# First mixer of a two-layer graph transformer: two heads' features by 64-row matmuls in turn, values with both halves as the stationary operand, and the next pair's key projection inside a pair

## The chip, the cores and the metric

The kernel runs on one core of one Trainium2 chip. The metric is the device time of one execution, in microseconds (us). Five engines work beside each other, each through its own list of instructions: PE (TensorE: matmuls; PEld is its weight load), DVE (VectorE), ACT (ScalarE), POOL (GpSimd) and SP (SyncE, which here only issues DMAs). They meet at semaphores. PSUM, into which PE writes, has eight banks.

## The reference, cut to what matters

625 nodes of 768 features pass through two layers, each of a graph network plus a mixer, and then a mixture of eight experts. The change touches only the first layer's mixer:

```python
xn = layernorm(x)                                    # 625 x 768
qkv = (xn @ W_qkv + b_qkv).reshape(b, n, 3, 12, 64)  # q, k, v: 12 heads of 64
q, k = q / 8, k / 8
phi_q = relu(einsum('bhnd,md->bhnm', q, random_features))   # 256 features
phi_k = relu(einsum('bhnd,md->bhnm', k, random_features))
kv   = einsum('bhnm,bhnd->bhmd', phi_k, v)
attn = einsum('bhnm,bhmd->bhnd', phi_q, kv) / 256
out  = attn.reshape(b, n, 768) @ W_proj + b_proj
```

## The kernel before, in words

**Arithmetic.** Every float32 product is made of three matmuls on two-part operands: a value is split in a high part (rounded by the write to the fp32r type) and a low part (the rest), and `mm3` (L582 to L588) adds high×high (L584), high×low (L587) and low×high (L588). So each operand is made by two engines in turn: ACT writes the high part out of PSUM, DVE subtracts it for the low part. Weights are split in a like way by POOL in this stage: `split` (L756) waits for the raw weights' DMA and until PE has used the unit two before (semaphore `unit_used`), writes the high part (L764) and then the low part (L766), which raises `unit_ready`. There are two buffers for units.

**The stage.** Nodes are five tiles of 128 (the last has 113 rows). XT holds the normalised rows transposed. The values of all heads are made first, in ten products of 18 matmuls, and kept as node rows in `attnT` (L1397, L1403, L915). Then a loop runs over six pairs of heads; a pair is 128 columns of q and of k. For each pair PE does, in this order (L2143 on):
- the projections of keys and queries: 4 × 18 matmuls with 320 moving columns, out of two weight units of 128 columns (2j and 2j+1; it waits for both before it begins), into banks 0 to 3. Then it tells POOL with `used(2)` (L2053) that both are free;
- for head s = 0, 1: the features of the keys (5 tiles × 3 matmuls, 256 columns each, banks 4 and 5) and of the queries (4 × 3 matmuls, 320 columns, banks 0 to 3). The random features are stored per head with zeros in the other head's 64 rows (`rfT[:, s, :]`), so that every matmul is one of 128 rows;
- `key_values`: phi_k (stationary, 128 nodes × 128 features) times the values of both heads (128 moving columns), for 2 feature halves × 5 tiles × 3 matmuls; of the result only the head's own 64 columns are kept;
- `attention`: 2 × 2 × 3 matmuls of 320 columns per head into banks 6 and 7; head 0's stand among head 1's features, head 1's at the end of the pair.

ACT and DVE follow each with its high and low part. In the names of the trace, `xt<-` and `weight<-` are the operands of a projection, `rfT` and `kT` (or `qT`) of the features, `attnT` and `phi_k` of key_values, `phi_qT` and `kv` of attention.

**What POOL does meanwhile.** The edges of the graph are sorted in this stage. DVE computes each edge's place (`pos_i`, L1375); after it, POOL goes through L802 on: it splits one 128-column unit, then issues eight indirect DMAs (L806) that scatter 125 edges each, then the next unit, until 80 scatters are done (behind the tenth unit); units 10 and 11 follow. Then it splits the two units of the output projection (`U_PROJ`). The sorted edges are read back by SP after the last scatter (L674).

**After the loop** PE waits for the last pair's `attnT` low part (L1438), does the output projection (`products(PR_PROJ, ...)`, 10 tiles × 18 matmuls of 384 columns), then the graph network.

Of the kernel before, what the change touches and what calls it, by code (L numbers as in the profile page):

```python
# [121 lines left out]
def build(nc, a, out):  # L122
    with ExitStack() as ctx:
# [67 lines left out]
        XN = er("xn_rows", [P, TILES, DIM], F32)  # L191
        rf2 = er("rf2", [P, 2, P], F32)
        rfT = er2("rfT", [P, 2, FEATS])
# [7 lines left out]
        with ExitStack() as here:  # L201
            srt, _ = allocator(here)
            src_i = srt("src_i", [EDGE_ROWS, EDGE_COLS], I32)
# [27 lines left out]
        with ExitStack() as here:  # L231
            mx, mx2 = allocator(here)
            attnT = mx2("attnT", [P, KD, COLS])
            qT = mx2("qT", [P, COLS])
            kT = mx2("kT", [P, COLS])
            v_f = [mx(f"v_f{s}", [P, WCOL], F32) for s in range(2)]
# [328 lines left out]
        FREE_A, FREE_B, FREE_C = 4, 2, 2  # L565
# [24 lines left out]
        def at(pair, *idx):  # L590
            return pair[0][idx], pair[1][idx]

# [47 lines left out]
        def _(sp):  # L640
# [115 lines left out]
        def _(pool):  # L756
# [31 lines left out]
            for part in rfT:  # L788
                pool.memset(f32(part[:, :, :]), 0.0).then_inc(consts, 1)
            pool.wait_ge(consts, 16)  # L790
# [25 lines left out]
            def expert_rows(n):  # L816
# [11 lines left out]
                pool.wait_ge(consts, 16 + 9 * (n + 1))  # L828
# [46 lines left out]
        def _(act):  # L875
# [28 lines left out]
            for s in range(2):  # L904
                own = slice(s * HEAD0, (s + 1) * HEAD0)
                act.activation(rfT[0][own, s, :], ps[own, RF_BANK, 0:FEATS], ACT.Copy).then_inc(rf_hi, 1)
            end_phase(act, "act", 1)

            act.wait_ge(consts, 16)
            act.dma_start(slot_rows_dram.rearrange("(s p) d -> p s d", p=P), zero_row[:, :].unsqueeze(1).broadcast_to([P, XSLOTS, DIM])).then_inc(cleared, 16)  # L910

            for j in range(SET):
                col, t = j // TILES, j % TILES
                act.wait_ge(prod_used, PR_V0 + j + 1)
                act.activation(attnT[0][:, 3 * col:3 * col + 3, t * P:(t + 1) * P], v_f[j % 2][:, :].rearrange("p (k n) -> p k n", k=3), ACT.Copy).then_inc(v_hi, 1)  # L915
            def key_features(j, s, n):
                t = slice(2 * n, min(2 * n + 2, TILES))
                w = t.stop - t.start
                act.wait_ge(B_full, 8 * j + 4 * s + n + 1)
                act.activation(phi_k[0][:, t, :], ps[:, 4 + n % 2, 0:w * FEATS].rearrange("p (t m) -> p t m", t=w), ACT.Relu).then_inc(B_hi, 1)  # L920

            def query_features(j, s, n):
                act.wait_ge(A_full, 12 * j + 4 * s + 2 * n + 6)
                act.activation(halves(phi_qT[0][:, n, :]), ps[:, 2 * n:2 * n + 2, 0:HALF], ACT.Relu).then_inc(A_hi, 2)

            with act.Fori(0, PAIRS) as j:
                for n in range(2):

                    act.wait_ge(A_full, 12 * j + 2 * n + 2)
                    act.activation(halves((kT, qT)[n][0][:, :]), ps[:, 2 * n:2 * n + 2, 0:HALF], ACT.Identity,  # L930
                                   bias=qk_bias[:, ds((1 - n) * KD + j, 1)]).then_inc(A_hi, 2)
                for s in range(2):
                    key_features(j, s, 0)
                    key_features(j, s, 1)
                    query_features(j, s, 0)
                    key_features(j, s, 2)
                    query_features(j, s, 1)
                    act.wait_ge(B_full, 8 * j + 4 * s + 4)
# [1597 lines left out]
```

## Time and profile before

| | us |
|---|---|
| three runs | 2519.56, 2531.16, 2527.87 |
| their median | 2527.87 |
| the profiled execution: own time | 2522.39 |
| its span in the trace | 2520.7 |
| mean granted clock of TensorE over the span | 0.935 of full |

The profiled execution lies 5.5 us below the median. Times in the trace count from the start of its span. A row of a timeline has: start, duration, engine, line, operation, output<-inputs, shapes, and in brackets the engine's idle time just before it with what ended it.

### The profile page before, as it was taken

To read this page: it belongs to the slowest core of one execution; us is meant where nothing else is said; L and a number is where in the kernel's file an instruction comes from. 1 tells how busy PE (TensorE), PEld (TensorE's weight loads), DVE (VectorE), ACT (ScalarE), POOL (GpSimd) and SP (SyncE) were. 2 spreads that over 40 slices of the span, in tenths; PEclk is the share of its full clock that TensorE was granted. 3 is DMA by queue.
4 is the path that set the end of the run, shared out by engine and by line. 5 is a ranking of instruction groups with operands and counts; after the bars stand their busy time and mean duration, and the time that the engine had idled before them with its cause. 6 is when DMAs were issued, how large, how long until landed. Compare 5 with 4: busy or idle time off the path is not lost. (4 is left out here: it accounts for less than half of the span.)

```text
span 2520.7 us, 33797 instructions
## 1 busy us (share of the span) xinstructions
PE 2216.7 (88%) x13346; PEld 2117.9 (84%) x13346; DVE 1408.4 (56%) x2284; ACT 942.0 (37%) x1250; POOL 500.7 (20%) x256
## 2 busy tenths in 40 slices
PE   5899999999999999999869919868888868999995
PEld 4899999999999999999858819767778857999995
DVE  7533455554555133333458863257984576888885
ACT  1222246666333011112126612214512223776772
POOL 4885510000300443443010012201110001000001
PEclk9899999999899999999969969988889977999997
DMA  3411223332322111110159951100112027999995
GB/s 99 133 26 52 69 86 128 112 125 93 140 94 85 57 51 44 38 57 20 48 176 308 299 194 38 63 28 30 53 59 84 13 91 266 350 348 360 346 338 186
DMA packets 158185, 326.79 MB, mean 130 GB/s; under 512 B 14096, under 2 KB 99296, under 8 KB 158042
## 3 DMA queue, kind: packets, MB, share of 16 engines
q1 hardware_dynamic: 133354, 265.68, 30.8%
q10 hardware_dynamic: 18928, 43.27, 4.8%
q0 software_dynamic: 5760, 15.86, 2.0%
q8 instruction: 98, 1.61, 0.3%
q14 instruction: 45, 0.37, 0.0%
HBM read 278.19 MB, written 46.51 MB: 129 GB/s over the span
## 5 line engine op out<-in xcount | busy, mean ns | idle before, releaser
L584 PE MATMUL banks<-weight_hi,xt_hi 128*128 128x384 f32 (+2 forms) x2208 | 740.9, 336 | 56.7 <-DVE xt_lo L1299 11.8
L587 PE MATMUL banks<-weight_lo,xt_hi 128*128 128x384 f32 (+2 forms) x2208 | 723.4, 328 | 0.0
L588 PE MATMUL banks<-weight_hi,xt_lo 128*128 128x384 f32 (+2 forms) x2208 | 723.0, 327 | 0.0
L584 PEld LDWEIGHTS banks<-weight_hi,xt_hi 128*128 128x128 f32 x2208 | 427.7, 194 | 72.9 <-issue 19.6
L587 PEld LDWEIGHTS banks<-weight_lo,xt_hi 128*128 128x128 f32 x2208 | 427.7, 194 | 0.4 <-issue 0.2
L588 PEld LDWEIGHTS banks<-weight_hi,xt_lo 128*128 128x128 f32 x2208 | 427.2, 193 | 0.0
L1704 DVE TENSOR_TENSOR weight_lo<-weight_raw,weight_hi 128x2304 fp32r<-128x2304 f32 (+2 forms) x153 | 342.5, 2243 | 89.3 <-ACT weight_hi L1039 89.3
L1039 ACT ACTIVATE weight_hi<-weight_raw 128x2304 fp32r<-128x2304 f32 (+2 forms) x153 | 287.0, 1879 | 71.4 <-PE banks L584 46.1
L764 POOL TENSOR_TENSOR weight_hi<-weight_raw,zero_col 128x2304 fp32r<-128x2304 f32 (+1 forms) x36 | 120.0, 3333 | 771.0 <-PE banks L584 334.3
L2220 PE MATMUL banks<-held_hi,a_rel 128*128 128x384 f32 x550 | 189.3, 344 | 0.6 <-DVE held_lo L1485 0.6
L2220 PE MATMUL banks<-held_lo,a_rel 128*128 128x384 f32 x550 | 187.6, 341 | 0.0
L584 PE MATMUL banks<-weight_hi,hT_hi 128*128 128x384 f32 (+1 forms) x442 | 151.2, 342 | 12.1 <-DVE hT_lo L1714 12.1
L1479 DVE TENSOR_TENSOR held_lo<-banks,held_hi 128x384 fp32r<-128x384 f32 x80 | 44.6, 557 | 209.5 <-ACT held_hi L977 209.5
L766 POOL TENSOR_TENSOR weight_lo<-weight_raw,weight_hi 128x2304 fp32r<-128x2304 f32 (+1 forms) x36 | 154.8, 4300 | 2.8
L588 PE MATMUL banks<-weight_hi,hT_lo 128*128 128x384 f32 (+1 forms) x442 | 149.7, 339 | 0.0
L587 PE MATMUL banks<-weight_lo,hT_hi 128*128 128x384 f32 (+1 forms) x442 | 149.7, 339 | 0.0
L866 POOL TENSOR_TENSOR weight_lo<-weight_raw,weight_hi 128x1536 fp32r<-128x1536 f32 (+2 forms) x16 | 70.3, 4393 | 350.6 <-ACT weight_hi L1100 350.6
L1467 DVE TENSOR_TENSOR adj<-adj,banks 128x640 f32 x80 | 65.4, 818 | 116.2 <-PE banks L2192 116.2
L977 ACT ACTIVATE held_hi<-banks 128x384 fp32r<-128x384 f32 x80 | 39.3, 491 | 242.2 <-PE banks L588 242.2
L853 POOL DMA_INDIRECT xt_hi<-slot_out,place x10 | 10.8, 1081 | 591.2 <-DMA slot_out<-bias_rows 588.8
L989 ACT ACTIVATE a_rel<-adj 128x640 fp32r<-128x640 uint16 x80 | 58.4, 744 | 173.1 <-PE banks L2220 173.1
L2220 PEld LDWEIGHTS banks<-held_hi,a_rel 128*128 128x128 f32 x550 | 105.3, 191 | 0.7 <-DVE held_lo L1485 0.7
(378 smaller groups left out, 4006.0 us busy)
## 6 DMA issues: line engine op xcount, KB each, us to landing
weight_raw<-L_ffn_w_in SPq DMA_DIRECT2D x102, 1152.0 KB, 6.4
weight_raw<-L_gnn_W_in SPq DMA_DIRECT2D x32, 1152.0 KB, 5.7
weight_raw<-L_ffn_W_in SPq DMA_DIRECT2D x17, 1152.0 KB, 7.3
products<-bias_rows SPq DMA_DIRECT2D x80, 192.0 KB, 1.9
slot_in<-slot_rows ACTq DMA_DIRECT2D x34, 384.0 KB, 6.2
slot_out<-bias_rows ACTq DMA_DIRECT2D x34, 384.0 KB, 5.8
weight_raw<-L_ffn_W_in SPq DMA_DIRECT2D x17, 576.0 KB, 6.2
product_back<-products SPq DMA_DIRECT2D x10, 960.0 KB, 4.7
```

The source lines that it names most:

```text
L584: ins = pe.matmul(dst, s[0], m[0], start=start, stop=False)
L587: pe.matmul(dst, s[0], m[1], start=False, stop=False)
L588: return pe.matmul(dst, s[1], m[0], start=False, stop=stop)
L764: pool.tensor_tensor(hi, raw[s][0:rows, 0:n], zero_col[0:rows, :].broadcast_to([rows, n]), ALU.add).then_inc(hi_ready, 1)
L766: pool.tensor_tensor(lo, raw[s][0:rows, 0:n], f32(hi), ALU.subtract).then_inc(unit_ready, 1)
L866: pool.tensor_tensor(lo, raw[u.slot][:, 0:n], f32(hi), ALU.subtract).then_inc(unit_ready, 1)
L989: act.activation(A_r[:, t, :, :], adj[:, r * TILES:(r + 1) * TILES, t * P:(t + 1) * P], ACT.Copy).then_inc(a_ready, 1)
L1039: act.activation(W4[u % RING][0][0:rows, 0:k * cols], RAW4[u % RAWS][0:rows, 0:k * cols], ACT.Copy).then_inc(e_hi[n], 1)
L1467: vec.tensor_tensor(block_of, block_of, ps[:, 2 * (s % 2):2 * (s % 2) + 2, 0:HALF], ALU.add).then_inc(slot_done, 1)
L1479: vec.tensor_tensor(lo[:, t, :], ps[:, part_bank(1, n), 0:WCOL], f32(hi[:, t, :]), ALU.subtract).then_inc(part_lo, 1)
L1704: vec.tensor_tensor(lo, RAW4[u % RAWS][0:rows, 0:k * cols], f32(hi), ALU.subtract).then_inc(e_lo[n], 1)
L2220: ins = pe.matmul(ps[:, agg_bank(m), 0:WCOL], A_r[:, t, src, :], part[:, src, :], start=(src == 0 and i == 0), stop=(src == FULL and i == 1))
```

## The change

1. `rfT` loses its zero halves (`[P, 2, FEATS]` becomes `[P, FEATS]`): the head s = 0 uses partitions 0 to 63, s = 1 uses 64 to 127, in matmuls of 64 rows. `heads3` issues them in turn: head 0, head 1, head 0, ... , each head into a bank of its own. Keys' and queries' features of both heads are read out together, by fewer and larger ACT and DVE instructions. Two memsets of POOL, one ACT and one DVE instruction go before the loop.
2. The values are stored so that one stationary operand of 128 columns holds head s's high half and low half side by side (`value_cols`). `keys_values` makes kv transposed, with phi_k as the moving operand: 2 heads × 5 tiles × 2 (phi_k high, phi_k low) matmuls of 256 columns. ACT copies the result out (512 columns), PE transposes it back by four 128×128 transposes, and DVE adds the parts and splits them (four instructions of 256 columns that wait for each other).
3. The order inside a pair is new, and written out instead of looped: the keys' projection of pair j+1 stands inside pair j, before the last two query features; the projection of the queries stands among the keys' features. Unit 2j is now the keys', 2j+1 the queries', each waited for by itself and freed by itself. POOL's list is as before.
4. XN moves to the part of SBUF that the sort uses; the wait counts on `consts` fall from 16 to 14.

```diff
-        rfT = er2("rfT", [P, 2, FEATS])
+        rfT = er2("rfT", [P, FEATS])
...
-            phi_k = mx2("phi_k", [P, TILES, FEATS])
-            phi_qT = mx2("phi_qT", [P, 2, COLS])
-            kv = mx2("kv", [P, 2, 2, P])
+            phi_k = mx2("phi_k", [P, 2, TILES, FEATS])
+            phi_qT = mx2("phi_qT", [P, 2, 2, COLS])
+            kv = mx2("kv", [P, 4 * P + 2 * HEAD0])
...
+        K_BANKS, Q_BANKS, F_BANKS, O_BANKS = slice(0, 2), slice(2, 4), slice(4, 6), slice(6, 8)
+        KEY_TILES = [slice(0, 2), slice(2, 4), slice(4, TILES)]
+        KEY_BANKS = [F_BANKS, K_BANKS, F_BANKS]
+        QUERY_BANKS = [F_BANKS, Q_BANKS]
...
-            with sp.Fori(0, PAIRS) as j:
+            for j in range(PAIRS):
                 for c in range(2):
-                    load(Unit(U_MIX + c, j, 2), qkv[:, :, c, ds(j * P, P)])
+                    load(Unit(U_MIX + 2 * j + c), qkv[:, :, 1 - c, j * P:(j + 1) * P])
... (ACT)
+            projection(0, 0)
+            for j in range(PAIRS):
+                for n in range(3):
+                    key_features(j, n)
+                projection(1, j)
+                act.wait_ge(B_full, 5 * j + 4)
+                act.activation(kvT_f, ps[:, O_BANKS.start, 0:2 * FEATS], ACT.Copy).then_inc(B_hi, 1)
+                for g in range(3):
+                    query_features(j, g)
+                if j + 1 < PAIRS:
+                    projection(0, j + 1)
+                query_features(j, 3)
... (DVE)
+            def keys_values(j):
+                of_hi, of_lo = kv_parts(O_BANKS.start + 1)
+                part = kv_part.rearrange("p (s m d) -> p s m d", s=2, m=2)
+                vec.wait_ge(B_full, 5 * j + 5)
+                order.step(vec.tensor_copy(part, of_lo))
+                order.wait()
+                order.step(vec.tensor_tensor(part, of_hi, part, ALU.add))
+                order.wait()
+                order.step(vec.tensor_copy(kv_own(kv[0]), part))
+                order.wait()
+                vec.tensor_tensor(kv_own(kv[1]), part, kv_own(f32(kv[0][:, :])), ALU.subtract).then_inc(B_done, 1)
... (DVE order: 3 key_features, projection(1, j), 2 query_features, keys_values, query_features, projection(0, j + 1), query_features, attention)
... (PE)
+            def heads3(bank, cols, of, by, unit_done):
+                for i, (a_of, a_by) in enumerate(((0, 0), (0, 1), (1, 0))):
+                    for s in range(2):
+                        own = slice(s * HEAD0, (s + 1) * HEAD0)
+                        ins = pe.matmul(ps[:, bank.start + s, cols], of[a_of][own], by[a_by][own], start=(i == 0), stop=(i == 2))
+                        if unit_done and i == 0 and s == 0:
+                            ins.then_inc(unit_used, 1)
+                return ins
...
+            def keys_values(j):
+                for s in range(2):
+                    for t in range(TILES):
+                        rows_of = slice(0, LAST if t == FULL else P)
+                        for h in range(2):
+                            ins = pe.matmul(ps[:, O_BANKS.start, s * FEATS:(s + 1) * FEATS], attnT[s][rows_of, j, t * P:(t + 1) * P],
+                                            phi_k[h][rows_of, s, t, :], start=(t == 0 and h == 0), stop=(t == FULL and h == 1))
+                            if s == 0 and t == 0 and h == 0:
+                                ins.then_inc(unit_used, 1)
+                ins.then_inc(B_full, 1)
...
+            for half in range(2):
+                projection(0, 0, half)
+            for j in range(PAIRS):
+                pe.wait_ge(A_done, 2 * j + 1)
+                if j > 0:
+                    pe.wait_ge(C_done, 5 * (j - 1) + 3)
+                key_features(j, 0, j == 0)
+                key_features(j, 1)
+                if j > 0:
+                    pe.wait_ge(C_done, 5 * (j - 1) + 4)
+                projection(1, j, 0)
+                pe.wait_ge(B_done, 4 * j + 1)
+                key_features(j, 2)
+                projection(1, j, 1)
+                if j == 0:
+                    pe.wait_ge(v_lo, SET)
+                else:
+                    pe.wait_ge(C_done, 5 * j)
+                pe.wait_ge(B_done, 4 * j + 3)
+                keys_values(j)
+                pe.wait_ge(A_done, 2 * j + 2)
+                query_features(j, 0)
+                query_features(j, 1)
+                pe.wait_ge(B_hi, 4 * j + 4)
+                for g in range(4):
+                    ins = pe.transpose(ps[:, O_BANKS.start + 1, g * P:(g + 1) * P], kvT_f[:, g * P:(g + 1) * P], ident[:, :])
+                ins.then_inc(B_full, 1)
+                if j + 1 < PAIRS:
+                    projection(0, j + 1, 0)
+                pe.wait_ge(C_done, 5 * j + 1)
+                query_features(j, 2)
+                if j + 1 < PAIRS:
+                    projection(0, j + 1, 1)
+                pe.wait_ge(C_done, 5 * j + 2)
+                query_features(j, 3, j + 1 < PAIRS)
+                pe.wait_ge(B_done, 4 * j + 4)
+                attention(j, 0)
+                pe.wait_ge(C_done, 5 * j + 4)
+                attention(j, 1).then_inc(C_full, 1)
+            pe.wait_ge(C_done, 5 * PAIRS)
             products(PR_PROJ, U_PROJ, lambda k: (attnT, k))
```

## Rows read from the trace of the kernel before

**Rows 1.** Busy time by stretch: us, then PE, PEld, DVE, ACT, POOL, granted clock, DMA
```profile
86.00:275.40 189.40, 177.46 (x1261) 172.19 (x1261) 59.43 (x92) 51.58 (x90) 135.70 (x96) 0.97 0.21 54
275.40:320.00 44.60, 43.85 (x251) 43.56 (x252) 21.61 (x25) 6.32 (x8) 22.09 (x5) 1.00 0.22 68
```

**Rows 2.** Timeline of ACT and DVE: keys of pairs 0, 4, 5; last result
```profile
93.69 0.80 ACT L930 ACTIVATE kT_hi<-banks,qk_bias 128x640 fp32r<-128x640 f32 x1 [8.89 <-PE banks L588]
217.60 0.80 ACT L930 ACTIVATE kT_hi<-banks,qk_bias 128x640 fp32r<-128x640 f32 x1 [4.58 <-PE banks L588]
247.65 0.80 ACT L930 ACTIVATE kT_hi<-banks,qk_bias 128x640 fp32r<-128x640 f32 x1 [4.58 <-PE banks L588]
274.50 0.82 DVE L1438 SCALAR_TENSOR_TENSOR attnT_lo<-banks,attnT_hi 128x640 f32 x1 [4.36 <-ACT attnT_hi L942]
```

**Rows 3.** Timeline of PE: first and last of four runs of one kind
```profile
99.83 0.28 PE L587 MATMUL banks<-rfT_lo,kT_hi 128*128 128x256 f32 x1
100.66 0.28 PE L588 MATMUL banks<-rfT_hi,kT_lo 128*128 128x256 f32 x1
103.14 0.22 PE L584 MATMUL banks<-attnT_hi,phi_k_hi 128*128 x1
106.33 0.27 PE L588 MATMUL banks<-attnT_hi,phi_k_lo 113*128 x1
146.59 0.41 PE L584 MATMUL banks<-phi_qT_hi,kv_hi 128*128 128x320 f32 x1 [0.77 <-DVE kv_lo L1434]
146.84 0.31 PE L587 MATMUL banks<-phi_qT_lo,kv_hi 128*128 128x320 f32 x1
150.29 0.31 PE L584 MATMUL banks<-xt_hi,weight_hi 128*128 128x320 f32 x1 [1.68 <-POOL weight_lo L766]
155.86 0.31 PE L588 MATMUL banks<-xt_hi,weight_lo 128*128 128x320 f32 x1
```

**Rows 4.** Timeline of POOL: splits and scatters of the loop
```profile
62.74 4.59 POOL L764 TENSOR_TENSOR weight_hi<-weight_raw,zero_col 128x768 fp32r<-128x768 f32 x1 [27.44 <-DVE pos_i L1375]
99.03 1.46 POOL L764 TENSOR_TENSOR weight_hi<-weight_raw,zero_col 128x768 fp32r<-128x768 f32 x1 [1.91 <-PEq L2053]
129.35 1.47 POOL L764 TENSOR_TENSOR weight_hi<-weight_raw,zero_col 128x768 fp32r<-128x768 f32 x1
192.81 1.46 POOL L764 TENSOR_TENSOR weight_hi<-weight_raw,zero_col 128x768 fp32r<-128x768 f32 x1 [0.75 <-PEq L2053]
222.50 1.19 POOL L806 DMA_INDIRECT edges_sorted<-code_i,pos_i  x1 [2.36 <-issue]
226.75 1.84 POOL L766 TENSOR_TENSOR weight_lo<-weight_raw,weight_hi 128x768 fp32r<-128x768 f32 x1
230.09 1.84 POOL L766 TENSOR_TENSOR weight_lo<-weight_raw,weight_hi 128x768 fp32r<-128x768 f32 x1
```

**Rows 5.** Granted clock in short stretches (columns as in rows 1)
```profile
86.00:88.00 2.00, 1.42 (x5) 1.42 (x6) 0.14 (x1) 0.00 (x0) 1.70 (x2) 0.50 0.99 334
178.00:182.00 4.00, 3.50 (x13) 3.51 (x14) 0.29 (x1) 0.04 (x1) 3.44 (x3) 0.57 0.05 13
```

**Rows 6.** Groups by line and form, 60 to 330 us: busy us, mean ns | idle
```profile
L1412 DVE SCALAR_TENSOR_TENSOR phi_k_lo<-banks,phi_k_hi 128x512 fp32r<-128x512 f32 x24 | 16.6, 691 | 17.8 <-ACT phi_k_hi L920 17.4
L924 ACT ACTIVATE phi_qT_hi<-banks 128x640 fp32r<-128x640 f32 x24 | 16.9, 705 | 9.1 <-PE banks L588 9.1
L1417 DVE SCALAR_TENSOR_TENSOR phi_qT_lo<-banks,phi_qT_hi 128x640 fp32r<-128x640 f32 x24 | 19.8, 824 | 8.2 <-ACT phi_qT_hi L924 7.8
L1412 DVE SCALAR_TENSOR_TENSOR phi_k_lo<-banks,phi_k_hi 128x256 fp32r<-128x256 f32 x12 | 5.0, 413 | 0.0
L584 PEld LDWEIGHTS banks<-attnT_hi,phi_k_hi 113*128 113x128 f32 x24 | 4.6, 192 | 0.1
```

**Rows 7.** Timeline before the loop (DVE) and at its start (PE)
```profile
32.54 0.88 DVE L1330 TENSOR_TENSOR rfT_lo<-banks,rfT_hi 64x256 fp32r<-64x256 f32 x2 [1.66 <-ACT rfT_hi L906]
...
86.58 0.63 PE L584 MATMUL banks<-xt_hi,weight_hi 128*128 128x320 f32 x1 [6.09 <-DVE attnT_lo L1403]
```

More of the change, by code:

```diff
@@ L922, in query_features @@
[L922 to L938, printed above, removed]
-                    act.activation(kv[0][:, :, s, s * HEAD0:(s + 1) * HEAD0], ps[:, 5, 0:2 * P].rearrange("p (m d) -> p m d", m=2)[:, :, s * HEAD0:(s + 1) * HEAD0],
-                                   ACT.Copy).then_inc(B_hi, 1)
-                act.wait_ge(C_full, 2 * j + 2)
-                act.activation(attnT[0][:, ds(j, 1), :].rearrange("p k (h n) -> p (k h) n", h=2), ps[:, 6:8, 0:HALF], ACT.Copy,
-                               scale=MIX0_SCALE).then_inc(C_hi, 1)
@@ L1326, in _ @@
             transposes_lo(TR_0)
[L1327 to L1330 removed]
+            vec.wait_ge(rf_hi, 1)
+            order.step(vec.tensor_tensor(rfT[1][:, :], ps[:, RF_BANK, 0:FEATS], f32(rfT[0][:, :]), ALU.subtract))
             vec.wait_ge(edges_in, 48)
@@ new lines, in _, with projection @@
+                    hi, lo = [value_cols(col, t, h) for h in range(2)]
+                    vec.tensor_tensor(lo, by_head(v_f[m % 2]), f32(hi), ALU.subtract).then_inc(v_lo, 1)
+            def projection(n, j):
+                t = (kT, qT)[n]
+                vec.wait_ge(A_hi, 2 * j + n + 1)
+                vec.scalar_tensor_tensor(halves(t[1][:, :]), ps[:, (K_BANKS, Q_BANKS)[n], 0:HALF], qk_bias[:, (1 - n) * KD + j:(1 - n) * KD + j + 1],
+                                         halves(f32(t[0][:, :])), ALU.add, ALU.subtract).then_inc(A_done, 1)
@@ new lines, in _ @@
+            projection(0, 0)
+            for j in range(PAIRS):
+                for n in range(3):
+                    key_features(j, n)
+                projection(1, j)
+                for g in range(2):
+                    query_features(j, g)
+                keys_values(j)
+                query_features(j, 2)
+                if j + 1 < PAIRS:
+                    projection(0, j + 1)
+                query_features(j, 3)
+                hi, lo = [halves(t[:, j, :]) for t in attnT]
+                vec.wait_ge(C_hi, 5 * j + 5)
+                vec.scalar_tensor_tensor(lo, ps[:, O_BANKS, 0:HALF], MIX0_SCALE, f32(hi), ALU.mult, ALU.subtract).then_inc(C_done, 1)
@@ L2163, in _, with projection @@
-            pe.wait_ge(C_done, FREE_C + 2 * PAIRS)
+            def projection(n, j, half):
+                u = U_MIX + 2 * j + n
+                pe.wait_ge(unit_ready, u + 1)
+                w = unit_view(u % 2, KD, P)
+                for k in range(KD):
+                    ins = mm3(pe, ps[:, (K_BANKS, Q_BANKS)[n].start + half, 0:HALF], at(w, slice(None), k), at(XT, slice(None), k, cols_half(half)),
+                              k == 0, k == KD - 1)
+                ins.then_inc(A_full, 1)
@@ new lines, in key_features, with query_features @@
+            def key_features(j, n, unit_done=False):
+                tiles = KEY_TILES[n]
+                for t in range(tiles.start, tiles.stop):
+                    i = t - tiles.start
+                    ins = heads3(KEY_BANKS[n], slice(i * FEATS, (i + 1) * FEATS), at(kT, slice(None), slice(t * P, (t + 1) * P)), rfT,
+                                 unit_done and i == 0)
+                ins.then_inc(B_full, 1)
+            def query_features(j, g, unit_done=False):
+                half, m = g // 2, g % 2
+                heads3(QUERY_BANKS[m], slice(0, HALF), at(rfT, slice(None), slice(m * P, (m + 1) * P)), at(qT, slice(None), cols_half(half)),
+                       unit_done).then_inc(C_full, 1)
```

172 lines of the change are left out of this document (58 added, 114 removed).

## The prediction

> **What bounds the kernel now.** I read the busy time by stretch first. The loop over the pairs of heads runs from about 86 to 275.4 us; PE is busy 177.5 of 189.4 us there, but POOL is busy too, 135.7 us, while DVE and ACT have less than a third [rows 1]. So there are two candidates, and the timelines have to tell which of them holds the end. After the loop PE is busy 43.9 of 44.6 us [rows 1]: what the loop gains is kept by what follows, since the weight splits there are released by PE's own progress.
>
> PE's pace: from pair 4's to pair 5's keys on ACT it is 247.65 − 217.60 = 30.05 us per pair [rows 2]. How that is made up comes from the starts of matmuls (their listed durations overlap). 39 rows of 320 columns in one run give 5.57 / 38 = 0.147 us from start to start; eight of 256 columns give 0.83 / 7 = 0.119; thirty of key_values, 128 columns, give 3.19 / 29 = 0.110 [rows 3]. From 320 to 256 columns 0.028 us go, so 128 columns would come to about 0.06; the 0.110 is a floor of another kind, which I read as the pace of the weight loads. A pair is then 72 × 0.147 = 10.6 (projections), 30 × 0.119 = 3.6 (key features), 24 × 0.147 = 3.5 (query features), 60 × 0.110 = 6.6 (key_values) and 24 × 0.147 = 3.5 (attention): 27.8, plus some 2.2 us of waits, such as the 0.77 for kv's low part [rows 3].
>
> POOL's pace: between the first splits of units 2 and 4 lie 129.35 − 99.03 = 30.3 us [rows 4], two splits and 16 scatters. It is nearly PE's pace. In the whole loop POOL waited for PE only 1.91 + 0.75 us; the other gaps, like the 2.36 at a scatter, have "issue" as their cause and are its own [rows 4]. In pair 2 PE waited 1.68 us for POOL [rows 3]. **So the two run neck and neck, and a faster PE meets POOL's list.** Unit 10 is ready at 226.75 + 1.84 = 228.6, unit 11 at 231.9 [rows 4].
>
> **The change part by part.**
> - *key_values.* 60 matmuls at 0.110 become 20 of 256 columns at 0.119: 6.6 − 2.4 = 4.2 us less per pair. Four transposes of 128 columns come: between the 0.110 of a 128-column matmul and the 0.25 of a restart; nearer the first, 0.15 each, 0.6 us [rows 3].
> - *64-row matmuls.* Their number (54 per pair) and columns stay. No row has one of 64 rows in turn with another. The nearest: the 113-row matmuls of key_values, mixed with 128-row ones, keep the 0.110 pace [rows 3], so fewer rows alone neither cost nor save. I take the old prices, 7.1 us per pair. Below: the 0.110 pace, 5.9. Further below: both heads at once, half of 7.1. Above: each changeover costs what a restart after a wait costs, 0.25 instead of 0.147 [rows 3]; with some ten changes between 64 and 128 rows per pair, 1.0 us, which I count.
> - *Order.* The waits at the start of a pair (keys' features for kT's low part, POOL's signal through a drain) are covered by the attention and the next projection. PE alone would need 10.6 + 7.1 + 2.4 + 0.6 + 3.5 + 1.0 = 25.2 us per pair, some 5 less than now.
> - *ACT and DVE.* Same elements in fewer instructions. DVE per pair: 1.8 (projections), key features of 1024, 1024 and 512 elements at 1.08 ns each from 0.691 and 0.413 [rows 6], 2.9, query features 4 × 0.82, kv four of about 0.4, attention 0.8: about 10.4 us, hidden under 25. It costs only where a chain is open, at the end.
> - *POOL.* Its list in the loop is unchanged. Its two waits for PE go, 2.7 us, because key units are freed by each pair's last query features and query units by keys_values, at least 10 us before POOL asks. The sort starts a bit sooner: rfT's two instructions of 0.44 each on DVE and as many on ACT become one each, 0.8 us [rows 7]. The two memsets lie beside an early wait for DMA: nothing. Later PE's first projection may begin when the values' products are read, not 6.09 us after [rows 7]; that too is nothing at the end, since the loop is paced by POOL.
> - *SP.* The loads keep place, size and number; keys' and queries' columns change turns. Written out loops cost code loading; PE's other stages are written out and are busy: nothing. After the loop U_PROJ's first unit is freed in pair 4, its second at pair 5's keys_values, about 247 plus 9.2 us of split: before it is needed, 16 us into the projection.
>
> **What the path is then.** POOL gives unit 10 (pair 5's keys) at 228.6 − 2.7 − 0.8 = 225.1 and unit 11 at 228.4. PE, with unit 9 at 207.8 (half of 30.3 and the 2.1 us that the pause at a scatter lasts over the usual 0.3, before unit 10), does pair 4's query projection, the last key features, keys_values, two query features and transposes in 5.3 + 0.7 + 2.4 + 1.8 + 0.6 = 10.8 us and stands at 219; it then **waits 6 us in front of pair 5's key projection**. This wait takes the place of the gain. From 225.2: key projection 7.1 (after an idle of 6.09 us the same 36 matmuls went from 86.58 to ACT's 93.69, partly at half clock, instead of 5.3) [rows 2, 5, 7]; two query features 1.8; attention 3.5 and 0.3 for its last query feature; key features 2.9; query projection 5.3; key features of the last tile 0.7; keys_values 2.4; query features 1.8: 251.0. Then the open chain of the last pair, no next projection to cover it: ACT and DVE on a query feature 0.7 + 0.8 [rows 6], DVE's four steps for kv 2.0, two more query features on DVE 1.6, attention's last half 0.4 + 1.8, ACT and DVE on the result 1.6: 8.9. Some 13 changeovers at 0.1: 1.3. The loop ends at 261.2, against 274.50 + 0.82 = 275.3 [rows 2]: **14.1 us less**. The profiled execution (2522.4) would go to 2508.3; it lies 5.5 us under the median, so against 2527.9 I forecast 2513.8.
>
> A measurement of this kernel can tell about 0.5%, 12.6 us, from no change; the forecast lies just past it.
>
> **Rivals.**
> 1. *The heads really run at once.* Then 24 key and 24 query-feature matmuls and the last tile's between 225 and the end (42 in all, 5.6 us) halve: 2.8 us more, a gain of 17, 2511. Nothing in the trace speaks for it, since no 64-row matmul is there; nor against. In pairs before the last it only makes the wait for POOL longer. The Trainium skill, "TensorE: Matmul & The Clock Gate", Part 3, The mechanism, states that matmuls in different row groups overlap, starting about 4 ns apart; by it this rival is the case. Chance 0.2.
> 2. *Nothing to tell.* PE's changeovers cost more, or its clock falls. In 178 to 182 us the granted clock was 0.57 though PE was 3.5 of 4 us busy, right after key_values [rows 5]: half of the time at 1.2 instead of 2.4 GHz, without a real pause. With half-filled matmuls and a wait in each pair this can come twice more on the way from 225 to the end: 2 × 1.8 = 3.6 us; and changeovers at 0.35 instead of 0.1 add 13 × 0.25 = 3.3. The gain is 7: 2521. The skill, "TensorEngine Tiling (Array Packing)", Key Properties, says that a change of tiling mode drains TensorE, without a price; no row here shows one. Chance 0.28.
> 3. *POOL does not hold PE.* If the scatters went faster than I read, the end would be PE's: a start at 84 (part of the 6.09 us wait before 86.58 goes [rows 7]) + 1.8 for the half clock + 6 × 25.2 + some 7 of the last pair's open chain = 244, a gain of 31, 2497. Against it is POOL's unchanged list with hardly a wait [rows 4]. Chance 0.04.
> 4. *Slower: the changing halves break the overlap of weight load and matmul in the features.* Its place is `heads3`. A 64-row load for one half might wait for the other half's matmul; each of 54 matmuls per pair would then cost load and matmul one after the other, 0.19 + 0.28 = 0.47 instead of 0.13, 18 us per pair [rows 3, 6]. PE would need 43 us per pair and the loop end near 350: 75 us slower, 2603. The point from which it decides: the end passes 275 when a pair takes over 30.5 us of PE, that is 0.1 us more for each of the 54. The unbroken 0.110 pace with 113-row loads speaks against it [rows 3]. Chance 0.06.
>
> That the change does not do what it says can only be rival 1's half of it: "in turn" need not be "at once".
>
> **How the numbers follow.** The forecast has 0.42; with rival 1 (0.20), 2 (0.28), 3 (0.04), 4 (0.06) that is all. Of the forecast's own 0.42, some 0.11 falls short of 12.6 us, because it lies 1.5 us past that bound. Faster by over 0.5%: 0.31 + 0.19 + 0.04 = 0.54; within: 0.11 + 0.28 + 0.01 = 0.40; slower: 0.06. The range goes from rival 1's gain with the runs' own spread below the median (8 us, 2519.56 against 2527.87) to rival 2's with the 3 us above: 2503 to 2524, widened at the top to 2526 for a gain of 5. Rivals 3 and 4 are left out.
>
> **What the profile would show.** POOL's scatters and splits without a wait for PE in the loop, unit 11 split by 228.5. PE waiting for POOL's low part before key projections, the last time about 6 us until 225, and clock 0.5 to 0.6 right after it. Matmul starts in the features 0.12 to 0.15 us apart (rival 1: in pairs with next to nothing between; rival 4: 0.4 and more). keys_values 2.4 us. The last attnT low part ending near 261. From there on every stage the same length as before. I am wrong if PE waits for nothing at the pairs' borders, or if the loop's gain is taken back later by a transfer or split that does not move with PE.

## Result, and the profile after the change

| | before | after |
|---|---|---|
| median of 5 runs each, us | 2523.71 (2519.56 to 2531.16) | 2506.35 (2503.13 to 2508.38) |
| ratio, 95% interval | | 0.9925 [0.9904, 0.9947] |
| profiled execution: own time, span, us | 2522.4, 2520.7 | 2508.38, 2506.6 |
| end of the last attention result, us | 275.32 | 265.57 |

The kernel is faster by 0.75%, 17.4 us; forecast were 14.1 us and a median of 2513.8. Between the two profiled executions lie 2520.7 − 2506.6 = 14.1 us of span. That equality with the forecast is luck: the loop gave only 275.32 − 265.57 = 9.75 us. The rest came in stages that the change does not touch. One line's instructions, in the expert stage, before and then after (first and last start):

```profile
L1722 DVE COPY bias_rows<-banks x68: 545/548/558, 1325.4 to 2493.5; 128x384 f32<-128x384 f32 x68
```

```profile
L1765 DVE COPY bias_rows<-banks x68: 546/549/558, 1321.1 to 2479.4; 128x384 f32<-128x384 f32 x68
```

At its first copy the changed kernel is 4.3 us ahead, at its last 14.1. So in this pair of executions the unchanged stages took away 5.4 us of the loop's gain and gave 9.8 us back later. With the repeats below, the change gave 0.75%, 0.35% and 0.54%, and the stretch behind the loop is no shorter with it; what a single profile shows there is scatter. I therefore go by the end of the loop from here on, and by the medians only for the whole.

Busy time by stretch, after (columns as in [rows 1]):

```profile
86.00:265.60 179.60, 147.65 (x1041) 134.19 (x1039) 69.60 (x87) 48.26 (x66) 136.38 (x96) 0.91 0.24 61
265.60:310.30 44.70, 43.92 (x248) 43.63 (x249) 21.13 (x24) 6.33 (x8) 21.53 (x5) 1.00 0.19 57
227.00:229.00 2.00, 2.00 (x8) 2.00 (x9) 0.00 (x0) 0.00 (x0) 1.92 (x2) 0.50 0.45 80
258.00:260.00 2.00, 1.98 (x7) 1.98 (x8) 1.43 (x2) 0.00 (x0) 0.00 (x0) 0.50 0.70 161
```

PE was busy in all but 12 us of the loop [rows 1]; now 32 us of it are idle. POOL's busy time is the same, 136.4 against 135.7 us, in a loop 9.8 us shorter. The granted clock fell from 0.97 to 0.91. The stretch behind the loop is as full as before. Who is waited for at the borders of pairs is shown by PE's timeline, and POOL's has the other side:

```profile
194.34 0.43 PE L592 MATMUL banks<-xt_hi,weight_hi 128*128 128x320 f32 x1 [4.71 <-POOL weight_lo L794]
226.79 0.64 PE L592 MATMUL banks<-xt_hi,weight_hi 128*128 128x320 f32 x1 [6.91 <-POOL weight_lo L794]
227.49 0.47 PE L596 MATMUL banks<-xt_hi,weight_lo 128*128 128x320 f32 x1
227.76 0.47 PE L592 MATMUL banks<-xt_hi,weight_hi 128*128 128x320 f32 x1
```

```profile
82.37 1.46 POOL L792 TENSOR_TENSOR weight_hi<-weight_raw,zero_col 128x768 fp32r<-128x768 f32 x1 [0.49 <-PEq L2096]
220.58 1.19 POOL L832 DMA_INDIRECT edges_sorted<-code_i,pos_i  x1 [2.37 <-issue]
224.94 1.80 POOL L794 TENSOR_TENSOR weight_lo<-weight_raw,weight_hi 128x768 fp32r<-128x768 f32 x1
252.29 5.07 POOL L794 TENSOR_TENSOR weight_lo<-weight_raw,weight_hi 128x2304 fp32r<-128x2304 f32 x1
```

POOL goes from split to scatter to split, and PE waits 6.91 us for unit 10, which is ready at 224.94 + 1.80 = 226.74. Behind it matmuls of 320 columns start 0.27 us apart (227.49 to 227.76), not 0.147; in 227 to 229 us the granted clock was 0.50, 1.2 instead of 2.4 GHz. What came as forecast stops here. The start of the feature stage of pair 0 on PE, then DVE and PE at the end of the last pair:

```profile
93.86 0.39 PE L2151 MATMUL banks<-rfT_hi,kT_hi 64*128 64x256 f32 x2 [1.80 <-DVE kT_lo L1436]
95.14 0.28 PE L2151 MATMUL banks<-rfT_lo,kT_hi 64*128 64x256 f32 x2
95.26 0.28 PE L2151 MATMUL banks<-rfT_hi,kT_lo 64*128 64x256 f32 x2
95.47 0.41 PE L592 MATMUL banks<-xt_hi,weight_hi 128*128 128x320 f32 x1
95.72 0.31 PE L595 MATMUL banks<-xt_lo,weight_hi 128*128 128x320 f32 x1
```

```profile
253.65 0.43 DVE L1461 TENSOR_TENSOR value_rows<-banks,value_rows 128x256 f32<-128x256 f32 x1
254.10 3.40 DVE L1463 CAST kv_hi<-value_rows 128x256 fp32r<-128x256 f32 x1
257.54 0.42 DVE L1465 TENSOR_TENSOR kv_lo<-value_rows,kv_hi 128x256 fp32r<-128x256 f32 x1
264.75 0.82 DVE L1481 SCALAR_TENSOR_TENSOR attnT<-banks,attnT 128x640 fp32r<-128x640 f32 x1 [5.32 <-ACT attnT L973]
```

```profile
251.31 0.66 PE L2219 MATMUL banks<-ident,value_rows 128*128 128x128 f32 x4
258.02 0.63 PE L592 MATMUL banks<-phi_qT_hi,kv_hi 128*128 128x320 f32 x1 [3.98 <-DVE kv_lo L1465]
```

Three things are to be read. **First**, every row of the 64-row matmuls has "x2": two matmuls in one slot, and a slot starts 0.12 us after the one before (95.14 to 95.26), the distance of single matmuls in the kernel before. The two heads really run at once. **Second**, where the kind of matmul changes, the start comes 0.21 us after the last one instead of 0.12, and the one behind it 0.25 instead of 0.147: some 0.2 us for a changeover. **Third**, a DVE copy of 128x256 elements took 3.40 us. It ended at 257.50, just after POOL's low part (252.29 + 5.07 = 257.36). Everything that closes the loop stands behind that copy. The two steps ahead of it, 0.42 and 0.43 us beside the same low part, read PSUM.

### The profile page after: what moved, and what is told of

It reads as the page before. It is cut to its first block and busy times, and to the rows that moved or that the text cites. A ratio compares the mean times of both kernels' runs of the same rounds, so it can differ in the third digit from the quotient of the medians.

```text
span 2506.6 us, 32770 instructions
## 1 busy us (share of the span) xinstructions
PE 2184.9 (87%) x13130; PEld 2078.6 (83%) x13130; DVE 1419.2 (57%) x2277; ACT 939.0 (37%) x1225; POOL 501.1 (20%) x254
## 5 line engine op out<-in xcount | busy, mean ns | idle before, releaser
L879 POOL DMA_INDIRECT xt_hi<-slot_out,place x10 | 11.5, 1149 | 592.7 <-DMA slot_out<-bias_rows 590.2
```

## Experiments

Every ratio is against the kernel before, run in turn on the same chip. "End" is that of DVE's last attention result; what POOL and PE do in the loop starts from the sort's last step (pos_i), and that starts at 61.6 to 63.5 us in all profiles but one.

**1. The two kernels again**, unedited: `before_again` and `after_again`, and `after_again2` on another chip.

> The kernel before once more, unedited. Its loop ends at 275.3 within 1 us again; the stages behind it vary by some us from trace to trace if the surplus is chance. Time 2519 to 2531 us.

> The changed kernel once more, unedited, for a second trace. Theory (POOL's list of scatters and splits sets the loop's end): the loop ends at 265.6 us within 1, PE waits some 6.9 us for unit 10, and the kernel takes 2503 to 2509 us. The first trace shows 9.75 us gained in the loop and 4.4 us behind it, where nothing was changed: if that part is chance, this trace puts the stages behind the loop at another length, by some us either way; if the change itself shortens them, they stay 4 us shorter than before.

> The changed kernel a third time, unedited. So far its gain over the kernel before was 0.75% in one set of runs and 0.35% in another, while both traces of its loop ended 9.8 and 11.4 us before those of the kernel before. Theory: the gain is the loop's, some 10 us or 0.4%, and what is over that is chance between sets: ratio 0.994 to 0.997.

| | median, us (n) | ratio | end, us | span behind the end, us |
|---|---|---|---|---|
| before_again | 2519.45 (12) | 0.9994 [0.9982, 1.0006] | 274.82 | 2240.7 |
| after_again | 2512.59 (8) | 0.9965 [0.9952, 0.9978] | 263.87 | 2241.3 |
| after_again2 | 2510.61 (6) | 0.9946 [0.9926, 0.9966] | 266.52 | 2234.6 |

The slow copy is there in both repeats of the kernel after (3.42 us each time), and so is PE's wait of 6.90 us for POOL. The loop ends 8.3 to 11.5 us sooner than in the kernels before, while the medians gain 8.4 to 17.4 us. The loop's part is the steadier figure. Two expectations for after_again were missed: its loop ended 1.7 us sooner than 265.6, and its median lies above 2509. Behind the loop the first two profiles took 2245.4 (before) and 2241.0 us (after); the three here do not keep that difference, so nothing puts it down to the change.

**2. Is it POOL that holds the loop?** In both kernels POOL issues 6 scatters after each unit instead of 8, and the last 8 behind unit 11; SP loads the output projection's weights ahead of reading back the sorted edges.

```diff
-                    while begun < min(EDGE_COLS, (2 * j + c + 1) * 8):
+                    while begun < min(EDGE_COLS, (2 * j + c + 1) * 6):
...
+            while begun < EDGE_COLS:
+                pool.indirect_dma_start(...)
+                begun += 1
             split_rest(U_PROJ, 1, 2, UNIT)
```

> The same relief in the kernel before. Theory: PE and POOL ran neck and neck there, so only the 1.7 us wait in pair 2 goes: loop end 273 to 275, time 0 to 3 us less. Rival (POOL held the kernel before as well, by more than its one wait shows): 10 us or more less.

> The changed kernel with POOL relieved: six scatters after each unit's split in place of eight, the eight that are left after unit 11, and the projection weights loaded ahead of the reading back of the edges. Theory (POOL holds PE): POOL's pace falls from 15.2 to 12.3 us per unit, PE's own pace is the 22.6 us from pair 0's to pair 1's key features in the changed trace, so pair 5's key features come at 94.9 + 5 x 22.6 = 207.9 and the loop ends near 232, 33 us sooner: 2473 us. Rival (PE's or DVE's own chain sets the end): at most the 6.9 us wait goes, 2500 us or more.

Measured: before_pool6 2519.45 us (12 runs), ratio 0.9991 [0.9981, 1.0002], end 271.96. after_pool6 2492.91 us (4), ratio 0.9878 [0.9859, 0.9897], end 232.77. Against the unedited kernels of the same chip the edit takes 2.9 us from the loop of the one (274.82 to 271.96) and 31.1 us from that of the other (263.87 to 232.77). The kernel before keeps its pace of 30.07 us per pair, and POOL now waits 2.4 to 6.0 us for PE in every pair, so that pace is PE's own:

```profile
183.77 0.80 ACT L934 ACTIVATE kT_hi<-banks,qk_bias 128x640 fp32r<-128x640 f32 x1 [4.58 <-PE banks L588]
213.84 0.80 ACT L934 ACTIVATE kT_hi<-banks,qk_bias 128x640 fp32r<-128x640 f32 x1 [4.58 <-PE banks L588]
```

The bound did move from PE to POOL. It has not left POOL altogether: in after_pool6 the keys of pairs 1 to 3 come 22.55 us apart, but those of the last two pairs 24.1 and 24.5 us behind the ones before them, with PE waiting 1.29 and 1.69 us for units. Of 31.1 us the whole kernel got 19.7 (medians, 2512.59 to 2492.91; 2473 was expected): behind the loop PE now stands still, since the output projection's splits are queued on POOL behind the last 8 scatters. PE, DVE and POOL there (timelines of after_pool6):

```profile
245.43 0.66 PE L592 MATMUL banks<-weight_hi,attnT 128*128 128x384 f32 x1 [14.25 <-issue]
```

```profile
232.69 13.45 DVE L1354 TENSOR_TENSOR x_rows<-x_rows,bias_rows 128x768 f32<-128x768 f32 x5
```

```profile
233.66 1.90 POOL L836 DMA_INDIRECT edges_sorted<-code_i,pos_i  x1 [0.30 <-issue]
235.58 4.03 POOL L792 TENSOR_TENSOR weight_hi<-weight_raw,zero_col 128x2304 fp32r<-128x2304 f32 x1
239.69 5.64 POOL L794 TENSOR_TENSOR weight_lo<-weight_raw,weight_hi 128x2304 fp32r<-128x2304 f32 x1
```

The unit is ready at 245.33 and PE starts at 245.43; the page puts that wait to "issue". Beside the same splits DVE's five bias additions take 13.45 us instead of 4.42 (below).

**3. Why did DVE's copy take 3.40 us?** Here the kernel after is kept, but the three steps on kv read at least one operand from PSUM, where before two of them read and wrote SBUF alone:

```diff
-                order.step(vec.tensor_tensor(part, of_hi, part, ALU.add))
+                order.step(vec.tensor_tensor(kv_own(kv[0]), of_hi, part, ALU.add))
...
-                order.step(vec.tensor_copy(kv_own(kv[0]), part))
+                order.step(vec.tensor_tensor(part, of_lo, kv_own(f32(kv[0][:, :])), ALU.subtract))
...
-                vec.tensor_tensor(kv_own(kv[1]), part, kv_own(f32(kv[0][:, :])), ALU.subtract).then_inc(B_done, 1)
+                vec.tensor_tensor(kv_own(kv[1]), of_hi, part, ALU.add).then_inc(B_done, 1)
```

> The changed kernel with DVE's four steps for kv all reading PSUM: kv_hi is the sum written straight out of PSUM, and the step that copies SBUF to SBUF (L1463) goes. In the changed kernel's last pair that copy took 3.40 us instead of 0.29, ending with POOL's split of the projection weights; PE then idled 4.0 us and did attention at half clock. Theory (POOL's two-input SBUF instructions hold DVE's SBUF-only instructions): the last pair's chain has no step over 0.5 us, PE's wait falls from 4.0 to about 1 us, attention stays at full clock, and the loop ends 3 to 5 us sooner, at 260 to 262. Rival (DVE's step was long for another reason, such as its layout): a step of about 3 us stays and the end moves by less than 1 us.

Measured: 2505.65 us (6), ratio 0.9934 [0.9915, 0.9953], end 259.20, 6.4 us sooner than after (265.57), of which 1.0 is an earlier pos_i. DVE, and POOL beside it:

```profile
252.42 0.43 DVE L1461 TENSOR_TENSOR kv_hi<-banks,value_rows 128x256 fp32r<-128x256 f32 x1
252.88 0.42 DVE L1463 TENSOR_TENSOR value_rows<-banks,kv_hi 128x256 f32<-128x256 f32 x1
253.34 0.42 DVE L1465 TENSOR_TENSOR kv_lo<-banks,value_rows 128x256 fp32r<-128x256 f32 x1
258.38 0.82 DVE L1481 SCALAR_TENSOR_TENSOR attnT<-banks,attnT 128x640 fp32r<-128x640 f32 x1 [3.15 <-ACT attnT L973]
```

```profile
251.07 5.15 POOL L794 TENSOR_TENSOR weight_lo<-weight_raw,weight_hi 128x2304 fp32r<-128x2304 f32 x1
```

POOL's split runs over all four steps, and none is longer than 0.43 us. PE's wait for kv falls from 3.98 to 1.00 us, and its clock stays up (granted 1.00 in 254 to 258 us). So it is not POOL's work as such that holds DVE, but the two meeting in SBUF. The other pairs of the kernel after show the same: the copy takes 0.29 us in pair 4, where no split runs (0.68 in pair 0, beside a scatter), and in pairs 1, 2, 3 and 5 it ends 0.15 us after a split does, 1.28, 1.18, 0.81 and 3.40 us long. The Trainium skill, "SBUF — State Buffer", Who interferes with whom, states that DVE and GpSimd share a port pair that one of them holds exclusively for a whole instruction, and that DVE uses it in its two-port modes, which a copy can enter, or for a second SBUF input; the trace agrees, with 3.40 us for a copy and 0.42 for steps that read PSUM. The ratio, 0.9934, lies among those of the unedited kernel (0.9925 to 0.9965), so what the edit is worth is shown by the trace of the loop alone.

**4. Both together, and taken back one at a time.** In `after_early` the kv steps are those of 3; the output projection's splits stand ahead of the last 14 scatters; sorted edges are read back behind one more load. `after_early_held` is the same with the old kv steps. `after_early_one_head` is after_early with the matmuls of head 1 issued behind those of head 0:

```diff
-                    while begun < min(EDGE_COLS, (2 * j + c + 1) * 8):
+                    while begun < min(EDGE_COLS, min(2 * j + c + 1, 2 * PAIRS - 1) * 6):
...
             split_rest(U_PROJ, 1, 2, UNIT)
+            while begun < EDGE_COLS:
+                pool.indirect_dma_start(...)
+                begun += 1
... (one_head only)
-                for i, (a_of, a_by) in enumerate(((0, 0), (0, 1), (1, 0))):
-                    for s in range(2):
+                for s in heads:
+                    for i, (a_of, a_by) in enumerate(((0, 0), (0, 1), (1, 0))):
```

> POOL relieved and better ordered: six scatters after each of units 0 to 10, then unit 11, the two splits of the projection weights, and the 14 scatters that are left; the edges are read back behind the loads of the next weights; kv's steps read PSUM. The first relief ended the loop at 232.8 us but PE then waited 14.3 us, because the splits of the projection weights stood behind the last scatters. Theory: the loop ends at 230 to 233, the wait of 14.3 goes, and this takes 13 to 16 us less than the first relief, about 2478 us. Rival: the wait moves on, to the sorted edges or the next weights, and less than 8 us are gained over it.

> As after_early, with DVE's kv steps as in the changed kernel. Now POOL's splits of the projection weights fall on 212 to 231 us, over the last pair's kv steps at about 221. Theory (SBUF-only steps on DVE are held until POOL's instruction ends): one or both of the two steps take 1 to 5 us and the loop ends 2 to 6 us later than in after_early. Rival: no difference over 1 us.

> As after_early, with the 64-row matmuls ordered one head after the other instead of in turn. In turn, the trace starts two at a time: twelve of 256 columns per key group in pairs 0.12 us apart. Theory (only different halves of the rows overlap, and only between neighbours): a pair of heads has 27 + 20 steps instead of 15 + 12, so 12 x 0.119 + 8 x 0.147 = 2.6 us more per pair; the loop is 15 us longer, 2493 us. Rival (the queue of PE pulls them together whatever the order): under 4 us more.

| | median, us (n) | ratio | end, us |
|---|---|---|---|
| after_early | 2486.45 (5) | 0.9847 [0.9826, 0.9867] | 232.73 |
| after_early_held | 2481.58 (5) | 0.9833 [0.9811, 0.9854] | 238.72 |
| after_early_one_head | 2482.41 (6) | 0.9837 [0.9814, 0.9859] | 232.05 |

*Held.* DVE in after_early_held; POOL's low part ran from 225.23 to 230.26:

```profile
225.34 5.21 DVE L1469 TENSOR_TENSOR kv_lo<-value_rows,kv_hi 128x256 fp32r<-128x256 f32 x1
```

The hold is back, on another instruction, and the loop ends 6.0 us later. The total is not longer for it, because after_early loses most of that time further on; its own expectation (2478 us, the wait of 14.25 us gone) came true only in part. There DVE takes up the read-back edges in the middle of the output projection, and PE runs out of free banks behind it. The step is one of 0.24 us in the kernel after, and here it too is held by a POOL split, until 263.32:

```profile
258.29 5.03 POOL L794 TENSOR_TENSOR weight_lo<-weight_raw,weight_hi 128x2304 fp32r<-128x2304 f32 x1
258.35 5.07 DVE L1491 CAST srcl_f<-part_i 128x160 f32<-128x160 int32 x1
```

```profile
264.55 0.69 PE L592 MATMUL banks<-weight_hi,attnT 128*128 128x384 f32 x1 [6.06 <-DVE x_rows L1343]
```

In the held kernel that wait is 1.47 us, so 4.6 of the 6.0 us are paid there. The cast is held there too, at nearly the same time (259.13, 5.21 us), but PE comes to its wait 5.5 us later (264.01 instead of 258.49).

*One head.* I expected the heads to stop overlapping and the loop to be 15 us longer; the rival in the expectation is what came. PE in after_early_one_head, the same place as above:

```profile
93.90 0.39 PE L2155 MATMUL banks<-rfT_hi,kT_hi 64*128 64x256 f32 x1 [1.81 <-DVE kT_lo L1440]
94.24 0.28 PE L2155 MATMUL banks<-rfT_hi,kT_lo 64*128 64x256 f32 x1
94.25 0.39 PE L2155 MATMUL banks<-rfT_hi,kT_hi 64*128 64x256 f32 x2
94.47 0.28 PE L2155 MATMUL banks<-rfT_lo,kT_hi 64*128 64x256 f32 x2
95.30 0.41 PE L2155 MATMUL banks<-rfT_hi,kT_lo 64*128 64x256 f32 x2
95.51 0.41 PE L2155 MATMUL banks<-rfT_hi,kT_hi 64*128 64x256 f32 x1
```

Three rows have one matmul, nine have two, three have one again. Six matmuls of head 0 were issued ahead of head 1's first. The row at 94.25 begins 0.01 us after the third matmul, while matmuls of one head start 0.12 us apart: so its first is head 1's, which starts beside head 0's third, ahead of three matmuls issued before it, on the other half of the rows. (Its second is head 0's fourth, one slot later; from 94.47 on the two heads start together.) The pace is 22.9 us per pair against 22.56. The loop ends no later than in after_early, since there PE waits 1.28 and 1.60 us for POOL in the last two pairs and here it does not wait. The way the code writes "in turn" is hardly needed. The Trainium skill, "TensorE: Matmul & The Clock Gate", Part 3, The mechanism, states that matmuls of different row groups overlap, and the trace agrees (two per 0.12 us); it also states that matmuls start strictly in order, and here these rows differ from it.

**5. What do 64 rows give?** `after_full` is the kernel after with the padded rfT of 128 rows for the features, as before. `after_best` is after_early with the first five additions of the output projection ahead of the edges' decoding on DVE, which takes after_early's wait of 6.06 us away (one of 2.35 us is left, in the graph network's first products). `after_best_full` is that with 128 rows.

```diff
... (the two full kernels)
-        rfT = er2("rfT", [P, FEATS])
+        rfT = er2("rfT", [P, 2, FEATS])
...
-                        ins = pe.matmul(ps[:, bank.start + s, cols], of[a_of][own], by[a_by][own], start=(i == 0), stop=(i == 2))
+                        ins = pe.matmul(ps[:, bank.start + s, cols], of(s)[a_of], by(s)[a_by], start=(i == 0), stop=(i == 2))
... (the two best kernels)
             add_bias(X, bias_row[1])
+            order.wait()
+            add_products(PR_PROJ, X, units=1)
...
-            add_products(PR_PROJ, X)
+            add_products(PR_PROJ, X, first=1)
```

> The changed kernel with the features' matmuls at 128 rows again (random features stored per head with zeros in the other half, as in the kernel before); values, order and kv as changed. Theory: the two heads' 64-row matmuls run at once, and without that each pair of heads needs 15 x 0.119 + 12 x 0.147 = 3.5 us more of PE; but up to unit 10 this only shortens PE's waits for POOL, so the loop ends 2 to 3 us later (what stands behind unit 10) and the time rises by 2 to 3 us. Rival (no real overlap): nothing changes.

> As after_early, and DVE decodes the sorted edges only after the first five additions of the output projection. In after_early PE waited 6.1 us for those additions, which stood behind the reading back of the edges. Theory: that wait goes, the loop ends at 231 to 233, and this is the fastest kernel: 2477 to 2482 us. Rival: the wait comes back at the next weights' split, and under 3 us are gained over after_early.

> As after_best with the features' matmuls at 128 rows. With POOL relieved PE paces the loop, so the overlap should show in full. One head after the other cost only 0.33 us per pair in the trace (22.9 against 22.56), because PE ran matmuls of the other rows beside them whatever the order. Theory: at 128 rows nothing can overlap and a pair takes 3.5 us more, 26 us; the loop ends some 20 us later and the time is 2497 to 2502 us. Rival (no overlap in truth, only in how the trace lists starts): the pace stays at 22.6 us.

| | median, us (n) | ratio | end, us |
|---|---|---|---|
| after_full | 2515.62 (9) | 0.9963 [0.9947, 0.9979] | 274.03 |
| after_best | 2473.75 (5) | 0.9817 [0.9794, 0.984] | 230.56 |
| after_best_full | 2481.09 (5) | 0.9837 [0.9818, 0.9856] | 234.80 |

after_full does not answer the question cleanly. Its end is 8.5 us late (2 to 3 were expected), but the sort was late too, from 62.83 to 69.44; from there to the end it took 204.6 us, against 202.7 in after and 201.4 and 203.4 in its repeats. Only behind the last wait for POOL can the two be laid side by side: from PE's first matmul on unit 10 to the last pair's transposes 26.3 us, against 24.5, 23.8 and 24.6. So where POOL holds the loop the 64 rows are worth some 2 us. The delay of the sort lies mostly in a group of DVE's instructions before the loop. The same group in before, in after and in after_full:

```profile
14.76 11.47 DVE L1283 TENSOR_SCALAR xn_rows<-x_rows,mean_var,rstd 128x768 f32<-128x768 f32 x5
```

```profile
14.51 15.25 DVE L1313 TENSOR_SCALAR xn_rows<-x_rows,mean_var,rstd 128x768 f32<-128x768 f32 x5
```

```profile
15.54 20.00 DVE L1317 TENSOR_SCALAR xn_rows<-x_rows,mean_var,rstd 128x768 f32<-128x768 f32 x5
69.44 0.24 DVE L1409 SCALAR_TENSOR_TENSOR pos_i<-low_i,sub_i 125x80 int32<-125x80 int32 x1
```

It ends at 26.23, 29.76 and 35.54 us. POOL splits the values' weights beside it, and one of these splits ends 0.4 us ahead of each end: at 25.82, 29.35 and 35.13. DVE is held by two, three or four splits, and that differs from run to run: it took 11.47 us in after_again as well, and 15.25 in after_again2. Nothing in the edit touches it; after_best_full, with the same rfT, has its pos_i at 61.55.

Where PE holds the loop, the question has an answer. Keys on ACT in two middle pairs of after_best, then of after_best_full:

```profile
135.47 0.80 ACT L948 ACTIVATE kT_hi<-banks,qk_bias 128x640 fp32r<-128x640 f32 x1 [2.13 <-PE banks L596]
158.02 0.80 ACT L948 ACTIVATE kT_hi<-banks,qk_bias 128x640 fp32r<-128x640 f32 x1 [2.12 <-PE banks L596]
```

```profile
136.62 0.80 ACT L952 ACTIVATE kT_hi<-banks,qk_bias 128x640 fp32r<-128x640 f32 x1 [1.93 <-PE banks L596]
160.64 0.80 ACT L952 ACTIVATE kT_hi<-banks,qk_bias 128x640 fp32r<-128x640 f32 x1 [1.94 <-PE banks L596]
```

22.55 against 24.02 us per pair: 64 rows save 1.47 us, not the 7.1 / 2 = 3.55 of halved slots. The expectation (26 us per pair, a loop 20 us longer, 2497 to 2502 us) was missed, on the side of less. The ends lie only 4.2 us apart and the medians 7.3: after_best meets POOL again in its last pair (23.61 us, a wait of 0.81), and its sort came 1.8 us later. With 128 rows the change from features to projection costs nothing (PE in after_best_full; "x2" stands there for two matmuls one after the other, 0.24 us the two):

```profile
95.23 0.40 PE L2162 MATMUL banks<-rfT_lo,kT_hi 128*128 128x256 f32 x2
95.47 0.40 PE L2162 MATMUL banks<-rfT_hi,kT_lo 128*128 128x256 f32 x2
95.70 0.31 PE L592 MATMUL banks<-xt_hi,weight_hi 128*128 128x320 f32 x1
95.85 0.31 PE L595 MATMUL banks<-xt_lo,weight_hi 128*128 128x320 f32 x1
```

The other 3.55 − 1.47 = 2.1 us, over some ten changeovers per pair, are 0.2 us each, the figure read above from the starts (0.09 + 0.10). after_best is the fastest kernel, 1.8% faster than before and 36.9 us faster by median than after_again2 beside it. Of its 51.9 us less span than before, 275.32 − 230.56 = 44.8 are the loop's.

## Why the prediction was right, and where it was wrong

- **The number:** the median of 2506.35 lies in the range (2503 to 2526), 7.4 us below the forecast of 2513.8. The gain by medians, 17.4 us, is more than was forecast, the loop's own, 9.75, is less. That the total came as near as it did is luck; what follows is judged by the loop.
- **The bound moves from PE to POOL: right, and shown** by experiment 2 (2.9 us from the one kernel, 31.1 from the other). PE waited 6.91 us at the last border, forecast 6; clock 0.5 after it.
- **Unit 10 ready at 225.1: 226.74, 1.6 late.** POOL's two waits for PE went (2.7 us), as forecast, but a new one of 0.49 came at 82.37, and the sort was not 0.8 sooner: rfT's step did shrink, while the normalisation ahead of it took 15.25 instead of 11.47 us, so pos_i came at 62.83 instead of 61.6. Where it took 11.47 us in a kernel after, pos_i came at 62.46 (after_again) and 61.85 (after_kv_psum). "The sort starts a bit sooner" failed in part by what holds DVE there; the rest stays open.
- **Forecast, heads in turn at old prices: wrong; rival 1 was the case.** From 226.79 to the transposes of the last pair at 251.31 PE took 24.5 us, against 251.0 − 225.2 = 25.8 and the 1.3 of changeovers, 27.1. That is 2.6 less. Rival 1 put its overlap at 2.8, for 42 matmuls; the path that the prediction adds up has 12 + 24 + 6 + 12 = 54 of them there, 7.1 us, and half of that is 3.55. Changeovers at 0.2 instead of 0.1 take 1.3 back. That gives 2.25 of the 2.6; the remaining 0.35 is about the 0.3 put down for a wait on the last query feature, which did not come (the attention starts 0.24 us after it, at 236.10). **Rival 2** was right in its two halves and wrong in their size: changeovers cost more than I counted, though not 0.35, and the clock fell once more on the way, by an idle it had not named.
- **PE alone at 25.2 us per pair: 22.55** in after_best, that is 25.2 − 3.55 (halved slots) − 1.0 + 2.1 (changeovers) = 22.75. Against before's 30.05 these are 7.5 us: 4.2 − 0.4 from keys_values and transposes (four transposes, 151.22 to 151.63 in after_best), 1.5 from the 64 rows, and the rest, 2.2, is as much as the waits inside the pair that the order was to cover.
- **The last pair's open chain of 8.9 us: 14.3** (251.31 to 265.57). This is the term that failed most. "DVE's four steps for kv 2.0" were 4.8, as the copy was held by POOL's split of the output projection's second unit. That split lay beside kv in the kernel before too (its low part 266.27 to 271.37), but there ACT made the high part and DVE's one step read PSUM:

```profile
269.85 0.29 DVE L1434 TENSOR_TENSOR kv_lo<-banks,kv_hi 128x128 fp32r<-128x128 f32 x1 [1.92 <-ACT kv_hi L939]
```

The change made kv by steps from SBUF to SBUF. PE's idle of 3.98 us then brought the clock to half, and the attention's 24 matmuls started 0.267 instead of 0.147 us apart at first, some 2.2 us more. I had asked of that split only whether it comes in time, not whom it runs beside.
- **Sum:** +1.6 − 2.6 + 5.4 = +4.4, from 261.2 to 265.6. The gain of the loop was 9.75 us and not 14.1; unchanged stages made up the difference in the profiled execution, and by the three sets of medians the change is worth 0.35 to 0.75%.
- **Rival 3** (POOL does not hold PE) needed the list edited: then the loop did end at 230.6 to 232.8, below its 244. **Rival 4** (load and matmul one after the other) fell: slots of 0.12 us.

Open: why the later stages vary by several us between executions of equal code; no run was made for it. That DVE's hold before the loop is the same thing as that on the kv copy was seen in traces (11.47, 15.25 and 20.00 us), but no run took POOL's splits away from it.

## What to carry to other kernels

Before speeding up an engine, lay its pace beside that of every engine that feeds it: here the change's real worth, 7.5 us per pair, showed only when two scatters per unit were moved behind the loop. Look at what runs beside an open chain, not only at what it waits for: a DVE step from SBUF to SBUF can be held for as long as a GpSimd one lasts, and reading an operand from PSUM avoided it. And follow each gain to the next stage by a run; twice here a part of what the loop gained came back as a wait behind it.

## What the runs showed of the hardware that was not expected

- DVE steps that touch SBUF alone, beside a POOL split: 3.40 us for a copy of 128x256 (0.29 otherwise), 5.21 for a subtraction of the same size (0.42 otherwise), 5.07 for a cast of 128x160 (0.24 otherwise), 13.45 for five additions (4.42 otherwise). Reading PSUM: 0.42 and 0.43 beside the same split.
- 64-row matmuls on the two halves run at once, also when they are issued head after head; one of them then starts ahead of three that were issued before it. A changeover between 64 and 128 rows costs about 0.2 us, so that of 3.55 us per pair 1.47 were saved.
- After 4 to 7 us of idle, matmuls of 320 columns start up to 0.27 us apart (granted clock 0.50) instead of 0.147.
